# Nine-instruction row deviations, placed one by one, in a recurrent LayerNorm stage

## The reference, cut to what matters

```python
def _layernorm(x, w, bias):
    mu = jnp.mean(x, axis=-1, keepdims=True)
    var = jnp.mean(jnp.square(x - mu), axis=-1, keepdims=True)
    return (x - mu) * jax.lax.rsqrt(var + EPS) * w + bias

def step(h, _):
    h = h + 0.01 * jnp.tanh(h)
    h = h * jax.nn.sigmoid(h)
    h = _layernorm(h, ln_w, ln_b)
    h = jnp.einsum('bsc,dc->bsd', h, W) + b
    return (h, None)
x, _ = jax.lax.scan(step, x, None, length=N_ITERS)   # N_ITERS = 30
```

## Time and profile before

| | us |
|---|---|
| three runs | 3338.03, 3341.35, 3341.97 |
| their median | 3341.35 |
| the profiled execution, its own time | 3341.66 |
| its span in the trace | 3339.9 |
| VectorE busy in the span | 2915.5 |
| TensorE busy in the span | 3091.6 |
| GpSimd busy in the span | 1722.7 |

### The profile page before, as it was taken

One profiled execution on the slowest core, in us unless ns is written; L12 is line 12 of the kernel. 1 busy time (PEld: TensorE's weight loads), 2 busy tenths in 40 slices (PEclk: granted clock), 3 DMA queues, 4 the chain that ended last, 5 costly groups with the idle time before them and its releaser, 6 DMA issues. The chain is left out here.

```text
span 3339.9 us, 67477 instructions
## 1 busy us (share of the span) xinstructions
PE 3091.6 (93%) x16801; PEld 2062.9 (62%) x16801; DVE 2915.5 (87%) x8976; ACT 2377.9 (71%) x4988; POOL 1722.7 (52%) x1101
## 2 busy tenths in 40 slices
PE   7989986999998999999995799999999999999998
PEld 4666665888886777777774544444444444444446
DVE  5777776888887888888887799999999999999997
ACT  4666663444444777777776988888888888888883
POOL 2445444333332111121110388888888877777776
PEclk9999998999999999999996799999999999999999
DMA  4000000000000000000000255454555555454447
GB/s 129 16 16 16 19 13 14 1 0 0 0 0 17 14 13 9 13 13 13 9 6 3 81 182 176 174 174 176 177 177 177 177 177 177 177 177 176 172 173 239
DMA packets 135072, 290.04 MB, mean 87 GB/s; under 512 B 12081, under 2 KB 69601, under 8 KB 135009
## 3 DMA queue, kind: packets, MB, share of 16 engines
q1 hardware_dynamic: 118112, 280.89, 24.5%
q10 hardware_dynamic: 16896, 8.39, 0.9%
HBM read 278.88 MB, written 10.35 MB: 87 GB/s over the span
## 5 line engine op out<-in xcount | busy, mean ns | idle before, releaser
L1074 POOL TENSOR_TENSOR d_g<-d_g,d_rb 128x1024 f32<-128x1024 f32 x480 | 1120.6, 2369 | 380.6 <-DMA d_rb<-d_rstd_rows 380.2
L1253 PE MATMUL d_p_y<-d_g,d_w_main 128*128 128x512 f32 x1856 | 953.2, 595 | 0.1
L1267 PEld LDWEIGHTS d_p_gt<-ident,d_g 128*128 128x128 f32 x3840 | 436.6, 142 | 710.2 <-ACT d_g L1312 657.1
L1312 ACT ACTIVATE d_g<-d_th,d_bias 128x512 f32<-128x512 f32 x928 | 669.7, 722 | 182.1 <-DVE d_th L1132 174.7
L1139 DVE BATCH_NORM_STATS2 d_stats<-d_p_gt 128x6 f32<-128x256 f32 x1920 | 725.1, 419 | 23.1 <-PE d_p_gt L1267 23.0
L1132 DVE SCALAR_TENSOR_TENSOR d_th<-d_th,d_p_y 128x512 f32<-128x512 f32 x960 | 652.3, 680 | 14.2 <-ACT d_th L1308 7.9
L1267 PE MATMUL d_p_gt<-ident,d_g 128*128 128x128 f32 x3840 | 602.3, 280 | 64.9 <-ACT d_g L1312 23.1
L1308 ACT ACTIVATE d_th<-d_p_y,d_bias 128x512 f32<-128x512 f32 x928 | 622.0, 670 | 1.1 <-PE d_p_y L1253 1.0
L514 ACT ACTIVATE a_prob<-a_masked,a_neg_max 128x128 f32<-128x128 f32 x1024 | 327.4, 392 | 111.8 <-DVE a_neg_max L334 111.7
L434 PE MATMUL a_p_s<-a_k_heads,a_q_t 128*128 128x512 f32 x768 | 397.0, 599 | 0.6 <-DVE a_k_heads L310 0.6
L451 PEld LDWEIGHTS a_p_pv<-a_v_ones,a_prob_t 128*128 128x128 f32 x3072 | 375.1, 193 | 10.7 <-issue 10.3
(11 more groups left out here) (167 smaller groups left out, 4443.7 us busy)
## 6 DMA issues: line engine op xcount, KB each, us to landing
d_rb<-d_rstd_rows SPq DMA_DIRECT2D x480, 512.0 KB, 5.5
a_adj_in<-in_adj_dram SPq DMA_DIRECT2D x64, 256.0 KB, 2.8
out_dram<-d_out_sb ACTq DMA_DIRECT2D x32, 256.0 KB, 3.2
d_rstd_rows<-d_rstd_row SPq DMA_DIRECT2D x120, 16.0 KB, 1.4
m_w_sb<-in_L_ffn_w_dram SPq DMA_DIRECT2D x2, 512.0 KB
x_sb<-in_x_dram SPq DMA_DIRECT2D x1, 256.0 KB, 2.9
a_w_raw<-in_L_gnn_Wq_dram SPq DMA_DIRECT2D x2, 64.0 KB, 2.2
a_w_raw<-in_L_gnn_Wk_dram SPq DMA_DIRECT2D x2, 64.0 KB, 2.1
```

Of the source, the lines that this page charges most:

```text
L1074: nc.gpsimd.tensor_tensor(g[:, c, :], g[:, c, :], rb[:, buf, :], ALU.mult).then_inc(s_gs, 1)
L1253: nc.tensor.matmul(p_y[:, c % 2, cols(u)], w_main[:], g[:, c, cols(u)], start=True, stop=True).then_inc(s_y, 1)
L1267: ins = nc.tensor.transpose(p_gt[:, t * P:(t + 1) * P], g[:, c, t * P:(t + 1) * P], ident[:])
L1312: nc.scalar.activation(g[:, c, cols(u)], th[:, c % 2, cols(u)], ACT.Silu, bias=col).then_inc(s_g, 1)
```

## The change

The last two Newton steps' arithmetic is traded for another with fewer instructions: from the seed one cubic step (n = 2 to 5) and one square step (n = 6 to 8) replace three square steps. A constant factor of 3/8 is moved into the centred weights. The chain has 9 instructions instead of 11. They stand in three places of each slot instead of two, one instruction in each: after the first mix, after the first statistics, after the second statistics. `work` is moved from PSUM to a new SBUF tile, `newton_work`.

```diff
-    CHAIN, XCHAIN = 11, 12
+    CHAIN, XCHAIN, PLACES = 9, 12, 3
+    RSTD_SCALE = 3.0 / 8.0
...
+        newton_work = sb("newton_work", [P, GTILES])
...
-        v, work, v_x, work_x = (p_nw[:, n * GTILES:(n + 1) * GTILES] for n in range(4))
+        v, v_x, work_x = (p_nw[:, n * GTILES:(n + 1) * GTILES] for n in range(3))
...
+                    y, work = rstd[:], newton_work[:]
...
-                            ins = nc.vector.tensor_scalar(rstd[:].bitcast(I32), v.bitcast(I32), -0.5, MAGIC,
-                                                          ALU.mult, ALU.add)
-                        elif n % 3 == 2:
-                            ins = nc.vector.tensor_tensor(work, v, rstd[:], ALU.mult)
-                        elif n % 3 == 0:
-                            ins = nc.vector.scalar_tensor_tensor(out=work, in0=work, scalar=-0.5, in1=rstd[:],
+                            ins = nc.vector.tensor_scalar(y.bitcast(I32), v.bitcast(I32), -0.5, MAGIC, ALU.mult, ALU.add)
+                        elif n == 2 or n == 6:
+                            ins = nc.vector.tensor_tensor(work, v, y, ALU.mult)
+                        elif n == 3:
+                            ins = nc.vector.tensor_tensor(work, work, y, ALU.mult)
+                        elif n == 4:
+                            ins = nc.vector.scalar_tensor_tensor(out=work, in0=work, scalar=-10.0 / 3.0, in1=work,
+                                                                 op0=ALU.add, op1=ALU.mult)
+                        elif n == 7:
+                            ins = nc.vector.scalar_tensor_tensor(out=work, in0=work, scalar=-0.5 * RSTD_SCALE ** 2, in1=y,
                                                                  op0=ALU.mult, op1=ALU.mult)
                         else:
-                            ins = nc.vector.scalar_tensor_tensor(out=rstd[:], in0=work, scalar=1.5, in1=rstd[:],
+                            ins = nc.vector.scalar_tensor_tensor(out=y, in0=work, scalar=5.0 if n == 5 else 1.5, in1=y,
                                                                  op0=ALU.add, op1=ALU.mult)
...
-                    for n in range(4 * ((c - 6) % GC) + 2 * place, 4 * ((c - 6) % GC) + 2 * place + 2):
-                        if n < CHAIN and live_group(k):
-                            newton(k, q, n)
+                    n = PLACES * ((c - 6) % GC) + place
+                    if n < CHAIN and live_group(k):
+                        newton(k, q, n)
...
+                        newton_part(i, c, 0)
                         if live(s - 2):
                             statistics(s - 2, (c - 2) % CHUNKS, 0)
-                        newton_part(i, c, 0)
+                        newton_part(i, c, 1)
...
-                        newton_part(i, c, 1)
+                        newton_part(i, c, 2)
...
-                link(nc.vector.tensor_scalar(w_centred[:], w_centred[:], row_sum[:], float(np.sqrt(P)),
+                link(nc.vector.tensor_scalar(w_centred[:], w_centred[:], row_sum[:], RSTD_SCALE * float(np.sqrt(P)),
```

## The result

The changed kernel takes 3531.38 us (median of four runs, 3523.19 to 3533.62) against 3340.03 us for the kernel before beside it. The ratio is 1.057, with a 95% interval of 1.055 to 1.059: slower by 191 us, where 240 were forecast.

The account below looks back on a forecast made before the run. VectorE was taken to bound the recurrent stage. A group of 11.2 + 2.7 = 13.9 us against 12.03, times 116, gave +217 us; with +21 for bias adds, 3341.66 became 3580 us, range widened to 3440 to 3760.

Parts of the forecast that it names:

- VectorE bounds the stage: Recurrent stage before the change: VectorE is the limit, busy 391.40 of 400 us; a group takes 12.03 us.
- The second stream: Chain instructions with two SBUF inputs need the second SBUF stream and collide with GpSimd's scaling; this decides the sign.
- Held to the end of one scaling, then served: All five two-SBUF-input chain instructions wait for the current GpSimd scaling, 2.34 us each, to end; chance 0.80.
- the rival in which VectorE waits for the whole run: Four back-to-back GpSimd scalings hold a chain instruction up to 9.4 us; 4000 to 4300 us; chance 0.05.
- The sum of holds, 2.7 us a group: Waits in the chain, mainly n = 7 and n = 8: middle of 2.3 and 3.3 us a group.
- The base, 11.2 us: A group without holds: 8 x 1.265 + 9 x 0.10 + 0.16 us, a gain of 0.83 us a group.
- the 0.16 us carried over from before: Rest of the 12.03 us group, put down to the fourth slot's slower TensorE and the loop's branch.
- The bias adds, +21 us: First 16 iterations: GpSimd's bias add, 2.36 us, lengthens one run in four and catches n = 3; about 1.3 us each.
- A dependent neighbour costs more than a single instruction: Chain on VectorE: second of a pair costs 0.21 us start to start, a single instruction 0.09, taken as 0.10.
- The rival without holds: Two plain SBUF inputs don't meet GpSimd's reads, leaving the 96 us gain: 3245 us, 3235 to 3275; chance 0.12.
- The lower bound of the forecast's own range: Holds of 2.0 us throughout: 13.2 us a group, +136 + 10 us, given as 3485 us.
- The last forecast sign: In the changed profile, GpSimd's idle time before its runs grows to about 4.5 us.

Follow-up runs that it names:

- before_sbuf: The kernel before with only work moved from PSUM to SBUF, its eleven instructions and their order kept: 3672.0 us, ratio 1.101.
- ten_free: The changed kernel with ten chain instructions instead of nine, none reading two SBUF tensors: 3231.46 us, ratio 0.967 against the kernel before.
- pool_halves: The changed kernel with each GpSimd scaling cut in two instructions of 512 columns: 3429.77 us, ratio 1.027 against the kernel before.
- before_single: The kernel before, eleven instructions and PSUM work unchanged, but one instruction in each of three places of a slot: 3245.19 us, ratio 0.971.

## Why the prediction was right

The sign, the mechanism and the size held; the measured change is 0.8 of the forecast. By its steps:

- *VectorE bounds the stage*: it stayed the limit, at 399.79 of 400 us, so every hold was paid in full.
- *The second stream.* No row of before showed a two-input instruction held, and the argument from L334 and the mix was what the sign hung on. The reading of L299 was not exact: of its four instructions the first is the long one, 1.43 us from 231.91 to 233.34, though L238 starts 0.07 us after it, and the other three follow at 0.33 us each, so that row doesn't show who was first. before_sbuf and ten_free show the hold by location alone, in both directions: +330 and -300 us. The rule that the Trainium skill states in "SBUF — State Buffer", "Who interferes with whom" (two SBUF inputs contend with a GpSimd instruction that reads SBUF) agrees with the 2335 ns against 182 ns here.
- *Held to the end of one scaling, then served.* The holds end 0.09 us behind the next scaling's start and never last over 2335 ns in the changed kernel, which by itself rules out the rival in which VectorE waits for the whole run; pool_halves shows the same with shorter instructions.
- *The sum of holds, 2.7 us a group.* Measured over 2000 to 3200 us: (133.0 - 175 x 0.17) + (89.2 - 88 x 0.17) + (55.1 - 88 x 0.18) + (30.1 - 88 x 0.17) = 232 us in 88 groups, 2.6 us. That contains the bias adds, and the forecast 2.7 us didn't. Behind the last of them, over 2800 to 3400 us with 45 row copies, the lines are:

```profile
L1169 DVE SCALAR_TENSOR_TENSOR d_rstd<-d_newton_work,d_rstd 128x32 f32<-128x32 f32 x90 | 61.9, 687 | 0.0
L1166 DVE SCALAR_TENSOR_TENSOR d_newton_work<-d_newton_work,d_rstd 128x32 f32<-128x32 f32 x44 | 49.6, 1126 | 0.0
L1161 DVE TENSOR_TENSOR d_newton_work<-d_newton_work,d_rstd 128x32 f32<-128x32 f32 x45 | 25.7, 570 | 0.0
L1163 DVE SCALAR_TENSOR_TENSOR d_newton_work<-d_newton_work 128x32 f32<-128x32 f32 x45 | 7.5, 168 | 0.0
```

  By the same sum that is 106 us, 2.4 us a group. So this term was 0.3 us too large, 35 us in 116 groups, the largest part of the miss. The prediction had 2.3 us for groups that alternate and 3.3 for groups that don't, and took a value in between; the groups alternate, mostly, as worked out: of the chains between 2400 and 2800 us the short groups take 11.9 to 12.4 us and the others 13.9 to 17.2, and after a short one n = 3 is caught and lasts 1.1 us. n = 7 and n = 8 carry most, as said.
- *The base, 11.2 us.* This term was too large: 13.64 - 2.63 = 11.0 us, which is 8 x 1.265 + 9 x 0.10 without the 0.16 us carried over from before. That is 0.2 x 116 = 23 us of the miss. The 0.16 us is gone in before_single and ten_free too, which have no holds, so it isn't the holds that remove it; what it was made of stays open.
- *The bias adds, +21 us.* Up to 2760 us, where they stand, the same sum gives 2.8 us a group, 0.4 us more than behind them, some 25 us in 60 groups (the first iteration's four left out): the term held. It comes about otherwise than forecast: a group behind a bias add has not only n = 3 but n = 4 and n = 5 held, in 10 of the 88 groups, and in no other of them are these two held. Together the three terms miss by 35 + 23 - 4 = 54 us, and the forecast by 3580 - 3531 = 49. The beat alone gives the result: 3341.66 + 116 x (13.64 - 12.03) = 3528 us.
- *A dependent neighbour costs more than a single instruction*: before_single gains 97 us by the places alone. The Trainium skill, "VectorE: DVE Perf Modes" ("The DRAIN you can't avoid"), states that a semaphore after each instruction costs nothing extra. No run here leaves a semaphore out: before_single keeps the count and every wait, so it shows that the count isn't all that matters for instructions of 128x32, and not whether the wait or the need for the neighbour's result is what costs.

The rival without holds, 3245 us, was false in its condition, and its price some 25 us too high: ten_free, without holds and with one instruction more than the changed kernel, takes 3231, so nine instructions without holds would take some 3231 - 0.10 x 116 = 3220 us, an estimate. That before_single comes to 3245 us too is chance; it has eleven instructions. The lower bound of the forecast's own range adds up to 3341.66 + 136 + 10 = 3488 us, not 3485, which changes nothing. The last forecast sign, GpSimd's idle time growing to 4.5 us, came out at 578.0 us for 120 groups, 4.8 us.

## What to carry to other kernels

Where GpSimd runs tensor_tensor instructions on SBUF beside a busy VectorE, the place of a tiny operand decides more than the count of instructions: give every short VectorE instruction an input from PSUM, even at the price of one instruction more. Put dependent short instructions between long independent ones instead of side by side. Before counting what an instruction costs, ask which path it needs and who holds it at that moment; the same instruction cost 0 or 2.3 us by its phase.

## What the runs showed that was not expected

GpSimd's one-input tensor_scalar of 1023 numbers takes 2.84 us where its two-input tensor_tensor of 1024 takes 2.35, yet holds VectorE only for its first 1.1 to 1.4 us. And in that kernel VectorE was mostly not served at the boundary behind a bias add. Of eleven instructions issued inside one, nine were held on through the small tensor_tensor, to 1.08 to 1.14 us after the start of the next tensor_scalar, as here, where the hold ends at 2424.21:

```profile
2420.60 2.41 POOL L1086 TENSOR_TENSOR x_sb<-x_sb,d_bias_bc 128x1024 f32 x1
2421.65 2.56 DVE L1170 SCALAR_TENSOR_TENSOR d_rstd<-d_newton_work,d_rstd 128x32 f32<-128x32 f32 x1
2423.07 2.83 POOL L1078 TENSOR_SCALAR d_g<-d_g 128x1023 f32<-128x1023 f32 x1
```

The longest hold, 3.90 us, began 0.31 us before a bias add and spanned it the same way. Why VectorE is served between two scalings and mostly wasn't there stays open.

In ten_free the recorded durations of VectorE are longer than elsewhere, at 2500 us by about 0.19 us (a mix 0.86 instead of 0.67, a chain instruction 0.36 instead of 0.17), while the starts are as close as before:

```profile
2501.07 0.36 DVE L1163 SCALAR_TENSOR_TENSOR d_p_nw<-d_newton_work,d_p_nw 128x32 f32<-128x32 f32 x1
2501.16 0.86 DVE L1135 SCALAR_TENSOR_TENSOR d_th<-d_th,d_p_y 128x512 f32<-128x512 f32 x1
2501.76 0.93 DVE L1142 BATCH_NORM_STATS2 d_stats<-d_p_gt 128x6 f32<-128x256 f32 x2
```

From a mix to the next statistics it is 0.60 us, as in the earlier trace rows. And they grow along the stage; the mix over 1900 to 2000 us and over 3050 to 3150 us, with the same count in each:

```profile
L1135 DVE SCALAR_TENSOR_TENSOR d_th<-d_th,d_p_y 128x512 f32<-128x512 f32 x73 | 51.1, 700 | 0.0
L1135 DVE SCALAR_TENSOR_TENSOR d_th<-d_th,d_p_y 128x512 f32<-128x512 f32 x73 | 73.0, 1000 | 0.0
```

That VectorE never waits isn't enough to bring it about: in before_single it is busy for all of the 1100 us as well, and its mix averages 683 ns. The cause stays open. Durations here overlap and don't tell the cost; the steps from start to start do.
